# A step order in a fused two-block attention kernel: attention product and silu first, two statistics passes reordered

## What is computed

```
x = x + block0(gn(x))
x = x + block1(gn(x))
```

```
ctx = einsum('bnd,bne->bde', k, v)
out = einsum('bnd,bde->bne', q, ctx)
out = silu(out); out = einsum('bcxy,oc->boxy', out, out_w)
return chan_ln(out, g_out)
```

## Time and profile before

| what | value |
|---|---|
| runs shown | 313.87, 315.68 and 315.61 us, median 315.61 |
| profiled execution | 314.74 us, span 313.0 |
| TensorE | busy 254.9 us (81%), mean granted clock 0.973 |
| VectorE | 198.2 us (63%) |
| ScalarE | 150.9 us (48%) |
| GpSimd | 122.8 us (39%) |

### The profile page before, as it was taken

The page is one execution under the profiler, slowest core; times in us unless marked ns, Lnnn a source line. Parts: engine busy times, 40 slices in busy tenths (PEclk is TensorE's granted clock), DMA queues, the critical chain, the costliest instruction groups (busy, mean ns, idle before and its releaser), DMA issues. The chain is left out here.

```text
span 313.0 us, 13341 instructions
## 1 busy us (share of the span) xinstructions
PE 254.9 (81%) x5715; PEld 193.7 (62%) x5715; DVE 198.2 (63%) x648; ACT 150.9 (48%) x364; POOL 122.8 (39%) x311
## 2 busy tenths in 40 slices
PE   0349699639889699975789979979899989889995
PEld 0226477427578477764566757757787767567761
DVE  3798987408997457999697866564133322457674
ACT  0456784048973467765463526731433347522220
POOL 8235566007877517763341403311133321253200
PEclk9999999959999999999599979999999999999999
DMA  7730088962000510000008280923100000002112
GB/s 229 130 75 23 0 199 186 212 159 63 4 4 20 92 25 4 0 2 0 3 2 184 51 175 4 203 73 94 46 4 4 4 4 4 2 4 70 69 45 92
DMA packets 15883, 20.07 MB, mean 64 GB/s; under 512 B 4288, under 2 KB 9408, under 8 KB 15808
## 3 DMA queue, kind: packets, MB, share of 16 engines
q1 hardware_dynamic: 12256, 18.03, 24.3%
q10 hardware_dynamic: 3568, 1.18, 2.2%
HBM read 4.33 MB, written 2.30 MB: 21 GB/s over the span
## 5 line engine op out<-in xcount | busy, mean ns | idle before, releaser
L1091 PE MATMUL bank<-cin,tband 64*32 64x240 f32 (+2 forms) x3072 | 85.5, 368 | 10.8 <-DMA cin<-cin 5.3
L1091 PEld LDWEIGHTS bank<-cin,tband 64*32 64x32 f32 x3072 | 67.2, 107 | 27.9 <-issue 10.0
L905 DVE STREAM_TRANSPOSE cpos<-bank 128x256 f32<-128x256 f32 x96 | 36.5, 423 | 49.9 <-PE bank L1091 49.7
L580 ACT ACTIVATE tband<-tband,row_edge 128x96 f32<-128x96 f32 (+1 forms) x96 | 32.3, 394 | 37.2 <-POOL tband L416 35.3
L1087 PE MATMUL bank<-ident,rings 128*128 128x128 f32 x192 | 32.4, 297 | 19.3 <-ACT rings L519 8.1
L1087 PEld LDWEIGHTS bank<-ident,rings 128*128 128x128 f32 x192 | 22.7, 150 | 33.5 <-ACT rings L519 10.7
L857 DVE STREAM_TRANSPOSE cin<-bank 128x768 f32<-128x768 f32 x32 | 30.9, 974 | 9.4 <-PE bank L1091 9.4
L452 POOL TENSOR_SCALAR ring_v<-cpos,mask_b 128x512 f32<-128x512 f32 x30 | 20.8, 708 | 34.9 <-PE bank L1091 20.4
L416 POOL TENSOR_TENSOR tband<-taps,pw 128x320 f32<-128x320 f32 x24 | 17.7, 737 | 37.8 <-PE bank L1091 37.8
L519 ACT ACTIVATE rings<-bank,ln_b,ln_s 128x128 f32<-128x128 f32 x64 | 24.2, 465 | 12.4 <-POOL ln_b L404 12.4
L1091 PE MATMUL bank<-w1t,rings 128*32 128x192 f32 x512 | 25.2, 355 | 1.2 <-ACT rings L657 1.2
(11 more groups left out here) (131 smaller groups left out, 433.7 us busy)
## 6 DMA issues: line engine op xcount, KB each, us to landing
cin<-cin SPq DMA_DIRECT2D x48, 192.0 KB, 4.4
cin<-cin SPq DMA_DIRECT2D x40, 64.0 KB, 2.4
xin<-in_x_dram SPq DMA_DIRECT2D x4, 512.0 KB, 6.1
out_dram<-rings SPq DMA_DIRECT2D x16, 128.0 KB, 1.9
taps<-tap_rows SPq DMA_DIRECT2D x16, 60.0 KB
taps<-tap_rows SPq DMA_DIRECT2D x16, 36.0 KB
cin<-cin ACTq DMA_DIRECT2D x8, 64.0 KB, 2.9
rings<-in_L_conv_w_qkv_dram ACTq DMA_DIRECT2D x1, 192.0 KB, 6.8
```

The costliest lines, as they stand in the source:

```text
L580: last = a.activation(dst[:, :, 2 + e], dst[:, :, e], ACT.Copy, scale=row_edge[:, e:e + 1])
L905: last = v.transpose(cpos[n % NS // TS][:, :, :, g * CG:(g + 1) * CG], bank[2 * (n % 4) + q][:, 0:B * HH])
L1091: return t_.matmul(dst, stationary, moving, start=start, stop=stop, skip_group_check=True)
```

## The change

- TensorE, each step: attend(s-3) comes first, ahead of z_transpose(s-6) and project(s-4); before, it came behind them.
- VectorE, each step: silu(s-3) comes ahead of moments(s-4) and x1(s-6); before, behind them. ScalarE's and GpSimd's lists are the same as before.
- gn_scale is split: gn_read copies the second product's result out of the bank and signals a new semaphore, s_gnr; gn_scale computes. raw_q(0) and o_transpose(0) now wait for s_gnr. xg1 still waits for s_gn.
- Second pass (pairs 2 to 4): its variance moves from the end of step 10 to behind x1_stats of step 11, its read from the start of step 11 to between the two transposes conv_in of qkv1(0), its scale behind both, alone and no longer in the gaps of moments. Its first product stands behind project(7), its second behind qkv1(0).
- Third pass (pairs 5 to 7): the read stays where the whole was, the scale moves behind attn_div(2).

```diff
-GN1 = ((0, 2, 8), (2, 5, 10), (5, 8, 13))
+GN1 = ((0, 2, 8), (2, 5, 11), (5, 8, 13))
...
-            def gn_scale(c, b0, n, ps, work=None):
+            def gn_read(c, n, ps):
                 dve.wait_ge(s_gnp, 2 * c + 2)
-                link(v.tensor_copy(gtmp[:, 2, 0:n], ps[:, B:B + n]))
+                v.tensor_copy(gtmp[:, 2, 0:n], ps[:, B:B + n]).then_inc(s_gnr, 1)
+
+            def gn_scale(c, b0, n, work=None):
+                dve.wait_ge(s_gnr, c + 1)
                 rsqrt(gn_s[:, b0:b0 + n], gtmp[:, 2, 0:n], n, work)
...
                 begun = 0
-                for c, (i0, i1, at) in enumerate(GN1[:2]):
-                    if step == at + 1 + (c == 0):
-                        if 0 <= step - 4 < PAIRS:
-                            begun = XL - 1
-                            work[0:0] = [lambda xl=xl: tile_stats(PAIRS + step - 4, bank[5 + step % 2][:, :], xl)
-                                         for xl in range(begun)]
-                        gn_scale(2 + c, 2 * i0, 2 * (i1 - i0), gn_sums[c], work)
+                if 0 <= step - 3 < PAIRS:
+                    silu(step - 3)
+                if step == GN1[0][2] + 2:
+                    begun = XL - 1
+                    work[0:0] = [lambda xl=xl: tile_stats(PAIRS + step - 4, bank[5 + step % 2][:, :], xl)
+                                 for xl in range(begun)]
+                    gn_read(2, gn_images[0][1], gn_sums[0])
+                    gn_scale(2, *gn_images[0], work)
                 if 0 <= step - 4 < PAIRS:
                     moments(PAIRS + step - 4, bank[5 + step % 2][:, :], work, begun)
                 for left in work:
                     left()
-                if 0 <= step - 3 < PAIRS:
-                    silu(step - 3)
...
                     for p in range(2):
                         dve.wait_ge(s_qkv, 2 * (PAIRS + n) + p + 1)
                         conv_in(p, n, unit(p))
+                        if p == 0 and step == GN1[1][2]:
+                            gn_read(3, gn_images[1][1], gn_sums[1])
+                if step == GN1[1][2]:
+                    gn_scale(3, *gn_images[1])
                 if 0 <= n - 1 < PAIRS:
                     kv_mask(n - 1)
-                i0, i1, at = GN1[2]
-                if step == at:
-                    gn_variance(4, 2 * i0, 2 * (i1 - i0), gn_sums[2])
-                if step == at + 1:
-                    gn_scale(4, 2 * i0, 2 * (i1 - i0), gn_sums[2])
+                if step == GN1[2][2]:
+                    gn_variance(4, *gn_images[2], gn_sums[2])
+                if step == GN1[2][2] + 1:
+                    gn_read(4, gn_images[2][1], gn_sums[2])
                 if 0 <= n - 1 < PAIRS:
                     attn_div(n - 1)
+                if step == GN1[2][2] + 1:
+                    gn_scale(4, *gn_images[2])
...
             def raw_q(i):
-                pe.wait_ge(s_q1, i) if i else pe.wait_ge(s_gn, 4)
+                pe.wait_ge(s_q1, i) if i else pe.wait_ge(s_gnr, 4)
...
                 if n == 0:
-                    pe.wait_ge(s_gn, 5)
+                    pe.wait_ge(s_gnr, 5)
...
+                if 0 <= step - 3 < PAIRS:
+                    attend(step - 3)
                 if 0 <= step - 6 < PAIRS:
                     z_transpose(step - 6)
-                if step == GN1[1][2] + 1:
-                    gn_of_block1(1, 0)
                 if 0 <= step - 4 < PAIRS:
                     project(step - 4)
-                if step == GN1[1][2] + 1:
-                    gn_of_block1(1, 1)
-                if 0 <= step - 3 < PAIRS:
-                    attend(step - 3)
+                if step == GN1[1][2]:
+                    gn_of_block1(1, 0)
...
                 if 0 <= n < PAIRS:
                     qkv1(n)
+                if step == GN1[1][2]:
+                    gn_of_block1(1, 1)
```

More of the change, by code:

```diff
@@ L161, in conv_blocks_kernel @@
         gn_sums = bank[0], bank[4], bank[7]
+        gn_images = [(2 * i0, 2 * (i1 - i0)) for i0, i1, _ in GN1]
         s_x = [sem(f"x_quarter{n}_loaded") for n in range(4)]
@@ L184, in conv_blocks_kernel @@
         s_gnp = sem("gn_product_done")
+        s_gnr = sem("gn_sums_out_of_psum")
         s_gn = sem("gn_ready")
@@ L870, in _ @@
             gn_variance(0, 0, B // 2, bank[7])
-            gn_scale(0, 0, B // 2, bank[7])
+            gn_read(0, B // 2, bank[7])
+            gn_scale(0, 0, B // 2)
             dve.wait_ge(s_gn, 1)
@@ L893, in _ @@
                 if step == 2:
-                    gn_scale(1, B // 2, B // 2, bank[7])
+                    gn_read(1, B // 2, bank[7])
+                    gn_scale(1, B // 2, B // 2)
                     dve.wait_ge(s_ident, 1)
@@ L1028, in _ @@
                     k_max(step)
-                for c, (i0, i1, at) in enumerate(GN1[:2]):
-                    if step == at:
-                        gn_variance(2 + c, 2 * i0, 2 * (i1 - i0), gn_sums[c])
+                for c in range(2):
+                    if step == GN1[c][2]:
+                        gn_variance(2 + c, *gn_images[c], gn_sums[c])
                 if 0 <= n < PAIRS:
```

## The result

Median of the changed kernel: 319.31 us (318.7 to 321.21, 4 runs), beside 315.64 (313.87 to 316.12, 4 runs) for the kernel before on the same chip. The ratio is 1.0114, 95% interval 1.007 to 1.0159: slower by about 1.1%. The profiled execution took 319.35 with a span of 317.6. The forecast was 317.3 with a range of 313.0 to 321.0.

The account below looks back on a forecast made before the run. The prediction took TensorE to bound steps 4 and 5, and VectorE from 129.72 us to the end of step 8. Terms 3.5 + 0.9 + 1.2 - 3.05 = +2.55 on the profiled 314.74 gave 317.3 us, range 313.0 to 321.0.

Parts of the forecast that it names:

- loop's order, steps 4 to 10: First block's attention loop: new order on TensorE and VectorE delays the aggregation ending step 10 by 5.85 us.
- low clock, steps 8 to 10: TensorE idle before attend(6) lowers its clock, slowing step 9's product, transpose and projection: +1.2 us, bounds 0 and +2.4.
- second pass, with masks: Statistics of pairs 2 to 4: loss of 5.85 shrinks to +3.5 at qkv1(2), then GpSimd's v masks add +0.9 us.
- third pass: Statistics of pairs 5 to 7: TensorE's 2.25 us idle before o_transpose(0) goes and the clock may hold; together -3.05 us.
- Silu's wait of 1.56 behind k_exp: Loop steps 4 to 8: VectorE's silu waits 1.56 us per step for ScalarE's tanh; +5.1 us at step 8's end.
- Steps 9 and 10: Loop steps without k_exp: step 9 starts 4.9 us later, silu(7) idles 1.1 in step 10; loss reaches +5.85 us.
- The masks beside the chain: Second pass: GpSimd's two v masks of pair 0 stretch VectorE's scale-and-bias operations; +0.9 us, bounds 0 and 1.2.
- The loop gets shorter: Rival: projection leaves the loop's cycle, 0.9 us saved per step if silu's idle is under 0.4; 311 us, chance 0.12.
- The third pass gives nothing: Rival: in the third pass another wait, division or v of pair 3, replaces gn_b; 320.3 us, chance 0.15.
- The clock falls inside the loop: Rival: TensorE idles some 1.8 us in each of steps 5 to 8, lowering its clock; 321.5 us, chance 0.13.
- the case that I gave 0.52: Whole kernel: time within 1% (3.1 us) of before, neither under 312.5 nor over 318.8 us; chance 0.52.

Follow-up runs that it names:

- small fillers: Changed kernel plus 9, 7, 7 and 5 unread constant products in TensorE's idle stretches of steps 8 to 11; median 318.46 us, ratio 1.0126.
- passes and fillers: Kernel before with the new statistics passes, plus 5, 3 and 7 unread constant products ending steps 8 to 10 on TensorE; median 311.47 us, ratio 0.987.
- passes only: Changed kernel with the loop's two moves (TensorE's product, VectorE's silu) undone, both reordered statistics passes kept; median 311.92 us, ratio 0.9856.
- third pass only: Kernel before with only the third statistics pass in the new order (read, division, then scale); median 313.44 us, ratio 0.9935.
- silu first: Changed kernel with only TensorE's move undone: attention product back behind transpose and projection; median 320.31 us, ratio 1.0172.
- tanh ahead of k_exp: Changed kernel with ScalarE's tanh(s-3) moved from behind k_exp(s-1) to ahead of it; median 315.08 us, ratio 0.9924.
- the product first and silu late: Changed kernel with only VectorE's move undone: silu back behind the moments; median 321.07 us, ratio 1.0174.

## Why the prediction came out as it did

In one account, terms of the sum against the runs (us on the stretch):

| step of the prediction | forecast | measured | from |
|---|---|---|---|
| loop's order, steps 4 to 10 | +5.85 | +5.64 | small fillers minus passes and fillers, qkv1(2) |
| low clock, steps 8 to 10 | +1.2 | +1.66 | 2.40 (after) minus 0.74 (passes only) |
| second pass, with masks | -2.35 + 0.9 = -1.45 | -1.16 | passes only minus before, qkv1(2) |
| third pass | -3.05 | -3.11 | passes only; third pass only -3.09 |
| sum | +2.55 | +3.03 | after minus before |

The -1.16 holds 0.34 of clock: the first w1t products took 3.54 in the passes-only kernel, 3.88 before.

- **Silu's wait of 1.56 behind k_exp** was right: 1.58 five times, and turning ScalarE's queue round took 2.44 off by the end of step 8 and 3.76 in all. The shift at the end of step 8 was 4.63 rather than 5.1 (145.57 less 140.30, less 0.64 from ahead): step 6 got 0.31 shorter where I had +0.04. Its work between the waits fell from 5.03 to 4.66, and one small operation of the moments makes 0.36 of that: before, it ran beside a GpSimd mask and took 0.53 (0.37 in step 7), after it 0.17 in both. I had seen this and allowed 0.1 for all of it. Step 6 before, VectorE and GpSimd:

```profile
127.24 0.53 DVE L851 TENSOR_SCALAR lnw<-lmv 128x4 f32<-128x4 f32 x1
127.05 1.36 POOL L452 TENSOR_SCALAR ring_v<-cpos,mask_b 128x512 f32<-128x512 f32 x2
```

- **Steps 9 and 10** cost more than I gave: silu waits 0.58 and 1.23. In the kernel with small fillers, free of low clock, the aggregation ends 5.89 later than before, where I had 5.85: two errors of about half a us, this one and the 0.47 at the end of step 8, cancelled. That the loop's term came out so close is luck.
- **The low clock** was the worst-sized term, and the one I had bounded without a row. I placed it ahead of moments(5) only, with 0 to 2.4 as bounds. It did fall there (the moments waited 1.02), but after qkv1(0)'s start as well: 4.61 instead of 3.88. That half stood in no term. I had taken qkv1(0) as slow in both kernels, not as slower. I had also read 145 to 155 us of the kernel before as mostly idle on TensorE; by the earlier trace rows it was busy 3.96 of the last 5 us there, at the low clock.
- **The second pass** returned what was forecast ahead of qkv1(0): with small fillers qkv1(0) starts 3.56 later than before, forecast 3.65; at the low clock 4.70. Up to qkv1(2) it returned 1.16, where I had 1.45 with the masks.
- **The masks beside the chain:** two operations took 0.59 and 0.64 instead of 0.17, 0.89 together, with the two masks of 1.36 at 165.80 beside them; I took 0.9 from the earlier trace rows. The same pair showed again in the passes-only kernel (0.60, 0.64). That 0.9 came out was partly luck, as my 1.2, the upper bound, was a miscount: of the three stretched operations of the earlier trace rows only two ran beside the masks, and the third (179.71, 0.66) beside another GpSimd instruction (L416, 179.62, 0.74). The Trainium skill, "SBUF — State Buffer", section "SBUF: two separate sides", has a VectorE operation with two SBUF inputs, or in a two-port mode, and a GpSimd operation exclude each other for a whole instruction. The trace agrees: two masks, two stretched operations, and each of these ends with a mask (166.50 beside 166.49, 167.17 beside 167.16).
- **The third pass** was right to 0.06, seen in three kernels: the idle of 2.25 was for gn_b alone, and with it went the low clock of qkv1(4).
- **The rivals.** "The loop gets shorter" fell: its deciding idle of under 0.4 was 1.58 in every step, and even with tanh first it was 0.25 to 1.30. "The third pass gives nothing" fell. "The clock falls inside the loop" fell for steps 5 to 8 (1.00 in 100 to 145), where TensorE's idles were 0.95 to 1.68 and not the 1.8 that I had; the fall came in step 9, after the 2.83 idle. But its row was weaker than I took it: the idle of 1.84 in step 1, which left the clock up before the change, brought it down in two of the twelve profiles.
- **The total.** 317.3 was 2.0 under the measured median. 0.48 of it is the sum's error (the loop 0.21 too high, the clock 0.46 and the second pass 0.29 too low, the third pass 0.06 too high), 1.5 lies in stages that the change doesn't touch. The ratio, 1.0114, just passes the 1% that I called the limit between no change and slower: the case that I gave 0.52 was missed by a margin that the interval (1.007 to 1.0159) doesn't resolve.

## What to carry to other kernels

When an operation moves to the head of an engine's step, read what stands ahead of its producer in the producer's queue: here tanh was behind k_exp, and k_exp behind the same engine's last operation, so moving the consumer forward closed a cycle, and reordering the producing queue was worth 2.4 us in the loop and 3.8 with the clock behind it. A change made of parts should be timed in parts: the two passes alone gave -4.3 us, and the loop's order ate 7.3. Let a waiting engine wait for the first step of a chain (the sums' read), not for its end, if that is all it needs; and count the idle you make on TensorE twice, once as time and once as clock.

## What the runs showed of the hardware

- In the changed kernel the granted clock went to 1.2 GHz after an idle of 2.83 us, but only at 145.7, when the product at 144.30 had already run at full speed, and came back at 149.1. It stayed at the high level after the single idle of 1.48 before 150.72, and was low again from 155.9 to 162.7: it fell soon after an idle of 1.92, and another of 1.26 lay inside. With fillers of 2.27 us or less in these idles no window of 140 to 165 was under 1.00, and 2.4 us of the path came back.
- The length of the last idle doesn't decide it. The idle of 1.84 or 1.85 us in step 1 is in all twelve profiles: it was followed by 1.2 GHz in two (third pass only, silu first), where k_max(1) or k_max(2) came 1.2 to 1.3 us late, and in the other ten it was not. With tanh ahead of k_exp an idle of 2.07 and one of 1.91 left the clock at 1.00 until 157.5, and with the product first and silu late it fell at 151.0, inside an idle of 2.67. So the price of the low clock in one profile is that execution's.
- Forty filler records took 4.73 us, eighteen 2.27: some 0.12 us each, so a filler is easily made too long, and then it costs what it saves.
- Small VectorE operations of 0.17 us took 0.59 to 0.64 beside GpSimd's masks, in the three kernels that I read for it (the changed one, passes only, small fillers), as in another stage of the kernel before (0.63). One mask stretches one operation, up to the mask's end.
- The same instructions in a stage fed by DMAs took 65.9 to 70.7 us in one execution or another. A term of 1 to 3 us could be measured only between marks that leave that stage out.
